# A state-space mixer with routed experts: the first drive of each tile moved from VectorE to POOL, with four reorderings around it

## The chip, the core and the metric

The kernel runs on one core of one Trainium2 chip. The metric is the device time of one execution in microseconds. Three runs of the kernel before gave 1138.83, 1135.27 and 1141.03 us; the median is 1138.83. TensorE is called PE here, VectorE DVE, ScalarE ACT, GpSimd POOL and SyncE SP.

## The reference

Sixty-four images of 3 x 96 x 96 become 37 tokens of 256 numbers each (36 patches of 16 x 16, projected, and a class token). Then come a state-space mixer and an expert layer, each with a residual and a layer norm:

```python
h = tokens(x)
h = layernorm(h + mixer(h))
h = layernorm(h + experts(h))
```

The mixer projects each token to x and z of 512 channels, runs a causal convolution of 4 taps and silu over x, and takes from it a step width per channel (`delta = softplus(...)`) and 16 numbers B and 16 numbers C per token. Then for each of 16 states s and each channel d, along the tokens of an image:

```python
h[d, s] = exp(delta[d] * A[d, s]) * h[d, s] + delta[d] * B[s] * x[d]
y[d]    = sum over s of h[d, s] * C[s]   (+ D[d] * x[d], times silu(z[d]), then projected to 256)
```

The expert layer takes the sigmoid of 32 logits per token, sums it over 8 groups of 4 experts, keeps the best 4 groups, of their experts the best 8, and adds the weighted outputs of these and of a shared expert. All is computed in 32-bit floats.

## The kernel before

**Stages.** The mixer goes over 11 tiles of up to 6 images (222 tokens; the first tile has 4 images, 148 tokens). Behind it lies the experts' stage: 179 blocks of 128 rows, gathered by expert. The change touches the mixer alone.

**A tile.** For tile i a loop runs over s = 0 to 15, one state each; I call a step of it a slot, and g = 16 i + s counts them all. In each slot:
- PE spreads row B of state g + 1 and row C of state g over 128 partitions into a bank of PSUM (`spread`, L809), two slots ahead, once the read that used the bank is done;
- ACT copies the row B from PSUM to SBUF (`copy_b`, L1076) and computes the decays, exp(delta * A), into PSUM (`decays`, L1088);
- POOL multiplies delta * x (`du`) by row B (`drives`, L629), 128 x 888 numbers, into one of four buffers;
- DVE runs the recurrence in two halves (`scan`, L1371), then multiplies the state by row C (`reads`, L1383);
- PE adds the products up over the states (`add_up`, L827).

The drive of slot 0 is the exception: DVE computes it itself (L1358), from row B in PSUM, in slot 15 of the tile before, between its scans and its read.

**What runs beside the slots.** Each engine has a function `pieces(i, s)` that says which other work it does in slot s: for the next tile n = i + 1 ("front") the convolution, softplus and so on, for the tile before t = i - 1 ("back") the output projection, layer norm, router and the allocation of rows to experts. The order of each engine's instructions is just this loop, written out by hand; semaphores tie the engines together. What matters here:
- PE: `project_patches` of tile i + 2 in slots 11 and 12 (L734), `project_z` in 12 and 14 (L790), `add_x` in 13 (L816), the convolution's parts (L748) in 14, 15 and 0; in slots 2 and 3 `project_out` of tile t, which first puts the tokens themselves (the residual) into the bank with products by the identity (L838) and then adds the projection (L845).
- ACT: in slot 12 the tanh of z, the weights of tile t (`weights`, L1156), the load of the table for the logarithm (L1193), the copy of row B of slot 15, then the logarithm of softplus (`softplus_ln`, L1068) and a line for its series (L1064).
- DVE: the router in slots 8, 9 and 10, with a copy `glist` of the four best groups (L1463); in slot 13 the smaller part (L1334), the read, `silu_z` (L1389), `tokens` of tile i + 2 (L1276) and the larger sum (`softplus_large`, L1339), which waits for ACT's logarithm; in slot 14 `softplus_sum` (L1345), which waits for POOL's product of the series, and `delta_x` (L1350), which makes `du`.
- POOL: one or more scatters of rows to DRAM in most slots (L617, tiles 2 on), the allocation's first part in slot 12 (L569 to L573) and second part in slot 14 (twelve steps that wait for each other, L576 to L587; tiles 1 on), its closing steps in slot 15 (L601 to L606), and in slot 14 the product of the series (`multiply_series`, L636), which waits for the larger sum. In a slot POOL's order is: product of the series, drive of slot g + 2, then the rest.

Of the kernel before, what the change touches and what calls it, by code (L numbers as in the profile page):

```python
# [52 lines left out]
OWN = (0,)  # L53
# [56 lines left out]
def build(nc, x, w_tok, b_tok, cls_tok, pos, w_in_x, w_in_z, conv_w, conv_b, w_x, w_dt, b_dt, a_log, d_par, w_out,  # L110
          gate_w, experts, shared, out, pool_rows, y_rows, bases):
    with ExitStack() as ctx:
# [90 lines left out]
        glist = sb("glist", [HALF, 2, 8])  # L203
# [106 lines left out]
        own_drive = sem("own_drive")  # L310
# [80 lines left out]
        CLEARED = 11  # L391
# [5 lines left out]

        def by_pool(g):
            return g % STATES not in OWN

        def pooled(g):

            return sum(by_pool(n) for n in range(g))
# [110 lines left out]
        def _(pool):  # L514
# [22 lines left out]
            for buf in (glist, gsum):  # L537
                nc.gpsimd.memset(buf[:], -2.0).then_inc(cleared, 1)
# [82 lines left out]
            def drives(g):  # L621

                i = g // STATES
                pool.wait_ge(b_copied, pooled(g + 1))
                if g % STATES == 1:
                    pool.wait_ge(du_done, i + 1)
                if g >= DRIVES:
                    pool.wait_ge(scan_done, 2 * (g - DRIVES + 1))
                nc.gpsimd.tensor_tensor(cut(drive[g % DRIVES], i), cut(du[i % 2], i),  # L629
                                        b_row[pooled(g) % B_ROWS][:, None, 0:width(i)].broadcast_to([P, KI, width(i)]), ALU.mult  # L630
# [31 lines left out]
            for i in range(-1, TILES):  # L662
                for s in range(STATES):
# [5 lines left out]
                    if 0 <= g + 2 < STATES * TILES and by_pool(g + 2):  # L669
                        drives(g + 2)  # L670
                    pieces(i, s)
# [52 lines left out]
        def _(pe):  # L724
# [70 lines left out]
            def spread(g):  # L795
# [5 lines left out]
                if g == 1:  # L801
                    pe.wait_ge(own_drive, 1)
# [28 lines left out]
            def project_out(t, b):  # L831

                h, a = half(t), images(t) // 2
                if b == 0:
                    pe.wait_ge(z2_done, 2 * t + 2)
                to = K[0:h, b * DM:(b + 1) * DM]
                for m in range(KM):
                    nc.tensor.matmul(to[:, m * P:(m + 1) * P], h0[t % 3][:, m, b * a:(b + 1) * a, :].rearrange("p a t -> p (a t)"), ident[:],  # L838
                                     start=True, stop=False, skip_group_check=True)
# [61 lines left out]
            def pieces(i, s):  # L901
# [5 lines left out]
                if i == TILES - 1 and s == 2:  # L907
                    add_x(i)
                if back and s in (2, 3):
                    project_out(t, s - 2)  # L910
# [22 lines left out]
                if i + 2 < TILES:  # L933
                    if s in (11, 12):
                        project_patches(i + 2, s - 11)
# [77 lines left out]
        def _(act):  # L1013
# [56 lines left out]
            def copy_b(g):  # L1070
# [3 lines left out]
                if pooled(g) >= B_ROWS:  # L1074
                    act.wait_ge(drive_done, pooled(g) - B_ROWS + 1)
                nc.scalar.activation(b_row[pooled(g) % B_ROWS][:, 0:w], BC[(g - 1) % 2][:, 0:w], ACT.Copy).then_inc(b_copied, 1)  # L1076
# [82 lines left out]
            def pieces(i, s):  # L1159
# [30 lines left out]
                if back and s == (12 if front else 11):  # L1190
                    weights(t)
# [586 lines left out]
```

## Time and profile before

| | |
|---|---|
| runs | 1138.83, 1135.27, 1141.03 us |
| profiled execution, own time | 1138.67 us |
| its span, first to last instruction | 1136.8 us |
| busy, share of the span | PE 87%, DVE 82%, ACT 59%, POOL 70% |
| DVE's scans L1371 | 352, 350.6 us |
| POOL's drives L629 | 165, 308.0 us |
| DVE's drives L1358 | 11, 11.3 us |

A share is an average over two stages with different limits. DVE is at nine tenths or more through nearly all of the mixer (about 40 to 775 us), PE in the experts' stage. The times of single instructions come from the timeline, which gives for each its start, its length, what it writes and reads, and, in brackets, how long its engine stood idle before it and what ended that.

### The profile page before, as it was taken

Reading aid. Unit: us, or ns where it says so; the run is one execution under the profiler, and the core shown is the slowest. Engines: PE = TensorE matmul, PEld = TensorE weight load, DVE = VectorE, ACT = ScalarE, POOL = GpSimd, SP = SyncE. Lnnn points to the kernel's source line nnn. Section 1 sums busy time; section 2 is a strip of 40 time slices with the busy share of each in tenths; the row PEclk is TensorE's granted clock in tenths of the full one; section 3 lists DMA queues with packets and bytes.
Section 4 is the critical chain, followed back from the end, with each engine's and each line's share of the span. In section 5 each row is a group of like instructions: output and inputs, shape, how many; then the busy total and the mean of one; then the engine's idle time right before and its main releaser. Section 6 shows DMA issues by size and latency. Waiting matters only on the chain.

```text
span 1136.8 us, 16973 instructions
## 1 busy us (share of the span) xinstructions
PE 987.1 (87%) x4739; PEld 755.5 (66%) x4739; DVE 935.5 (82%) x1813; ACT 672.6 (59%) x1780; POOL 793.6 (70%) x840
## 2 busy tenths in 40 slices
PE   5698889989898998989989897866699999999990
PEld 5686667767676766667767673534488888888880
DVE  4589999999999999999999999895244677777774
ACT  3575665756557575666756657541266666666661
POOL 2244577878888787888878888786501776767775
PEclk9999999999999999999999998878699999999995
DMA  5699300201111020110201010058465888889983
GB/s 187 219 326 325 114 24 23 62 15 59 38 47 55 19 82 15 54 42 31 75 14 59 14 49 28 28 214 351 147 183 176 256 263 262 261 261 273 268 260 108
DMA packets 104475, 150.28 MB, mean 132 GB/s; under 512 B 13983, under 2 KB 91231, under 8 KB 103999
## 3 DMA queue, kind: packets, MB, share of 16 engines
q1 hardware_dynamic: 87487, 107.39, 29.5%
q0 software_dynamic: 16896, 41.80, 12.7%
q8 instruction: 40, 0.66, 0.2%
q14 instruction: 52, 0.43, 0.1%
HBM read 72.32 MB, written 76.82 MB: 131 GB/s over the span
## 4 chain that ended last, share of the span: by engine, by line
DVE 30%; PE 29%; issue 17%; ACT 5%; POOL 5%; DMA 4%; SPq 2%; DVEq 0%; POOLq 0%; ACTq 0%
DVE arena L1371 17%; PE BC L983 11%; DMA mixer_own<-pool_dram 3%; DVE arena L1383 3%; PE F L734 3%; PE Y L977 3%; PE K L997 3%; PE F L997 3%; PE Y L827 2%; POOL arena L629 1%; PE D L989 1%; POOL pool_dram L617 1%; ACT arena L1039 1%; POOL gat L685 1%; PE K L790 1%
## 5 line engine op out<-in xcount | busy, mean ns | idle before, releaser
L1371 DVE TENSOR_TENSOR_SCAN arena<-D,arena 128x444 f32<-128x444 f32 (+1 forms) x352 | 350.6, 1036 | 10.9 <-ACT D L1088 8.8
L827 PE MATMUL Y<-arena,ident 128*128 128x444 f32 (+1 forms) x704 | 304.3, 560 | 1.6 <-DVE arena L1383 1.6
L685 POOL DMA_INDIRECT gat<-y_dram,slot_all x176 | 177.4, 1008 | 124.6 <-DMA y_dram<-mixer_own 67.9
L617 POOL DMA_INDIRECT pool_dram<-hrow,slot_of x176 | 175.8, 999 | 45.8 <-issue 38.1
L629 POOL TENSOR_TENSOR arena<-mixer_own,arena 128x888 f32<-128x888 f32 (+1 forms) x90 | 164.2, 1825 | 56.9 <-ACT arena L1076 56.0
L1088 ACT ACTIVATE D<-mixer_own,aneg 128x216 f32<-128x216 f32 (+1 forms) x384 | 148.3, 427 | 79.7 <-DVE arena L1371 76.6
L1383 DVE TENSOR_TENSOR arena<-arena,BC 128x888 f32<-128x888 f32 (+1 forms) x176 | 184.8, 1050 | 5.4
L983 PE MATMUL BC<-arena,xt 128*128 x716 | 186.6, 384 | 0.0
L629 POOL TENSOR_TENSOR arena<-arena 128x888 f32<-128x888 f32 x75 | 143.8, 1917 | 53.0 <-ACT arena L1076 51.3
L827 PEld LDWEIGHTS Y<-arena,ident 128*128 128x128 f32 x704 | 127.5, 200 | 73.0 <-issue 68.1
L1088 ACT ACTIVATE D<-arena,aneg 128x216 f32<-128x216 f32 x320 | 126.9, 437 | 64.8 <-DVE arena L1371 64.8
L748 PEld LDWEIGHTS F<-h,arena 128*128 128x128 f32 x704 | 130.7, 197 | 28.8 <-issue 19.1
L748 PE MATMUL F<-h,arena 128*128 128x222 f32 (+3 forms) x704 | 140.2, 346 | 7.7 <-DVE h L1276 6.4
L1636 DVE SCALAR_TENSOR_TENSOR act_g<-tanh_g,BC 128x128 f32<-128x128 f32 x179 | 51.5, 288 | 107.3 <-ACT tanh_g L1224 105.8
L983 PEld LDWEIGHTS BC<-arena,xt 128*128 128x128 f32 x716 | 123.6, 193 | 9.9 <-issue 0.3
L809 PE MATMUL BC<-bc_rows,sel 96*128 96x222 bf16 (+1 forms) x352 | 63.6, 263 | 66.4 <-DVE arena L1383 66.4
L1076 ACT ACTIVATE arena<-BC 128x222 f32<-128x222 f32 (+1 forms) x165 | 56.8, 344 | 77.4 <-PE BC L809 76.4
L809 PEld LDWEIGHTS BC<-bc_rows,sel 96*128 96x128 bf16 x352 | 30.4, 98 | 98.5 <-DVE arena L1383 86.9
L977 PE MATMUL Y<-ident,mixer_own 128*128 128x128 f32 x358 | 70.0, 278 | 10.8 <-DMA mixer_own<-pool_dram 10.6
L1220 ACT ACTIVATE xt<-Y 128x256 f32<-128x256 f32 x179 | 67.4, 377 | 18.8 <-PE Y L977 18.6
L1224 ACT ACTIVATE tanh_g<-BC 128x128 f32<-128x128 f32 x179 | 49.6, 277 | 43.8 <-PE BC L983 43.8
L734 PE MATMUL F<-arena 128*128 128x216 f32 (+1 forms) x264 | 53.1, 355 | 23.4 <-ACT mixer_own L1040 8.8
(230 smaller groups left out, 1569.8 us busy)
## 6 DMA issues: line engine op xcount, KB each, us to landing
mixer_own<-pool_dram SPq DMA_DIRECT2D x179, 144.0 KB
y_dram<-mixer_own SPq DMA_DIRECT2D x179, 128.0 KB
pool_dram<-filler SPq DMA_DIRECT2D x5, 4176.0 KB, 32.0
arena<-in_experts_dram SPq DMA_DIRECT2D x1, 7680.0 KB, 23.0
arena<-in_x_dram SPq DMA_DIRECT2D x10, 648.0 KB, 4.3
pool_dram<-filler SPq DMA_DIRECT2D x1, 4896.0 KB, 35.6
arena<-in_experts_dram SPq DMA_DIRECT2D x1, 4608.0 KB, 16.1
pool_dram<-hrow,slot_of POOLq DMA_INDIRECT x176, 2.7
```

The lines of the kernel that those rows point to most:

```text
L617: nc.gpsimd.indirect_dma_start(out=pool_rows, out_offset=bass.IndirectOffsetOnAxis(ap=slot_of[q][0:r, b, k:k + 1], axis=0), in_=hrow[q][0: ...
L629: nc.gpsimd.tensor_tensor(cut(drive[g % DRIVES], i), cut(du[i % 2], i), b_row[pooled(g) % B_ROWS][:, None, 0:width(i)].broadcast_to([P, KI ...
L685: nc.gpsimd.indirect_dma_start(out=gat[0:r, k, b, :], out_offset=None, in_=y_rows[0:(blocks_by(t) - k) * P, :], in_offset=bass.IndirectOff ...
L734: mm = nc.tensor.matmul(F[:, m * np_:(m + 1) * np_], tokw[:, k, m * P:(m + 1) * P], cut_patches(patches, n)[:, k, :], start=(k == 0), stop ...
L748: nc.tensor.matmul(to.rearrange("p (a t) -> p a t", t=TOKENS)[:, :, back:], inw4[:, k, TAPS - 1 - back, c * P:(c + 1) * P], h0[n % 3][:, k ...
L809: mm = nc.tensor.matmul(BC[g % 2][:, j * N:j * N + w], sel[:, STATES * j + s, :], bc_rows[i % 2][:, 0:w], start=True, stop=True)
L827: mm = nc.tensor.matmul(Y[j][:, 0:w], ident[:], read[g % 3][:, j * w:(j + 1) * w], start=(s == 0), stop=(s == STATES - 1), skip_group_chec ...
L977: mm = nc.tensor.transpose(PX[b % 2][:, k * P:(k + 1) * P], xg[b % XG][:, k * P:(k + 1) * P], ident[:])
L983: mm = nc.tensor.matmul(PG[b % 2][:, 0:DM], xt[b % 2][:, k * P:(k + 1) * P], weights[k], start=(k == 0), stop=(k == KM - 1))
L1088: last = nc.scalar.activation(D[b][:, c * w:(c + 1) * w].rearrange("p (a t) -> p a t", t=TOKENS)[:, :, 1:TOKENS], cut(delta[i % 2], i)[:, ...
L1371: nc.vector.tensor_tensor_scan(state[g % 2][:, lo:hi], D[b][:, 0:hi - lo], drive[g % DRIVES][:, lo:hi], 0.0, ALU.mult, ALU.add).then_inc(s ...
L1383: nc.vector.tensor_tensor(cut(read[g % 3], i), cut(state[g % 2], i), BC[g % 2][:, None, N:N + width(i)].broadcast_to([P, KI, width(i)]), A ...
```

## The change

- All sixteen drives of a tile run on POOL. The one of slot 0 comes in slot 14 behind the product of the series and the second part of the allocation, and waits for `du`. ACT copies its row B too, first thing in slot 14; DVE's L1358 and its semaphore go, and its read of slot 15 now waits for that copy.
- The list for the group mask: no copy `glist`; the last four entries of `gtop` are overwritten with -2 by a memset on DVE and `gtop` itself is the list.
- DVE runs the larger sum of softplus ahead of `tokens` in slot 13.
- PE puts the residual's products of both halves into the bank in slot 0 (`add_tokens`), not in slots 2 and 3.
- The second `project_patches` goes from slot 12 to slot 13; on ACT the weights of tile t go from slot 12 to 13 and the copy of row B comes before the table load.

```diff
@@ POOL
             def drives(g):
                 i = g // STATES
-                pool.wait_ge(b_copied, pooled(g + 1))
-                if g % STATES == 1:
+                pool.wait_ge(b_copied, g + 1)
+                if g % STATES == 0:
                     pool.wait_ge(du_done, i + 1)
...
                     if i + 1 < TILES and s == 14:
                         multiply_series(i + 1)
-                    if 0 <= g + 2 < STATES * TILES and by_pool(g + 2):
+                    if s == 14:
+                        pieces(i, s)
+                    if 0 <= g + 2 < STATES * TILES:
                         drives(g + 2)
-                    pieces(i, s)
+                    if s != 14:
+                        pieces(i, s)
@@ PE
+            def add_tokens(t):
+
+                h, a = half(t), images(t) // 2
+                pe.wait_ge(z2_done, 2 * t + 2)
+                for b in range(2):
+                    for m in range(KM):
+                        nc.tensor.matmul(K[0:h, b * DM + m * P:b * DM + (m + 1) * P],
+                                         h0[t % 3][:, m, b * a:(b + 1) * a, :].rearrange("p a t -> p (a t)"), ident[:],
+                                         start=True, stop=False, skip_group_check=True)
...
+                if back and s == 0:
+                    add_tokens(t)
                 if back and s in (2, 3):
                     project_out(t, s - 2)
...
-                    if s in (11, 12):
-                        project_patches(i + 2, s - 11)
+                    if s in (11, 13):
+                        project_patches(i + 2, (s - 11) // 2)
@@ ACT
-                if back and s == (12 if front else 11):
+                if back and s == (13 if front else 11):
                     weights(t)
                 if front and s == 12:
-                    nc.scalar.preload_act_table_set("natural_log_exp_and_others")
                     if mix:
                         copy_b(STATES * i + s + 3)
+                    nc.scalar.preload_act_table_set("natural_log_exp_and_others")
                     softplus_ln(n)
@@ DVE
                 if b == 0:
-                    if by_pool(g):
-                        dve.wait_ge(drive_done, pooled(g + 1))
-                    else:
-                        dve.wait_ge(own_drive, g + 1 - pooled(g + 1))
+                    dve.wait_ge(drive_done, g + 1)
...
-                in_turn(nc.vector.tensor_copy(glist[0:h, :, 0:TOPG], gtop[0:h, :, 0:TOPG]))
+                in_turn(nc.vector.memset(gtop[0:h, :, TOPG:], -2.0))
                 for b in range(2):
                     hold()
-                    last = nc.vector.match_replace(gleft[0:h, b, :], glist[0:h, b, :], gsum[0:h, b, :], -1.0)
+                    last = nc.vector.match_replace(gleft[0:h, b, :], gtop[0:h, b, :], gsum[0:h, b, :], -1.0)
...
+                if front and s == 13:
+                    softplus_large(n)
                 if i + 2 < TILES and s == 13 and mix:
                     tokens(i + 2)
-                if front and s == 13:
-                    softplus_large(n)
...
-                    if 0 <= g + 1 < STATES * TILES and not by_pool(g + 1):
-                        drives(g + 1)
                     if 0 <= i < TILES:
                         reads(g)
```

## Rows read from the trace of the kernel before

**Rows 1.** Busy us per engine by stretch: length, PE, PEld, DVE, ACT, POOL, granted clock, DMA.

```profile
492.00:560.00 68.00, 62.04 (x286) 46.02 (x285) 66.14 (x96) 43.14 (x111) 56.88 (x60) 0.97 0.15 45
800.00:1137.00 337.00, 300.18 (x1613) 247.42 (x1611) 206.22 (x702) 194.16 (x559) 199.23 (x202) 0.95 0.77 228
```

**Rows 2.** Timeline of DVE, one tile's slots 8 to 15: start, us, what, idle before.

```profile
467.69 0.94 DVE L1463 COPY glist<-gtop 111x8 f32<-111x8 f32 x1
...
491.18 2.29 DVE L1339 SCALAR_TENSOR_TENSOR arena<-arena,ln_small 128x888 f32<-128x888 f32 x1 [0.30 <-ACT arena L1068]
...
496.65 1.14 DVE L1345 SCALAR_TENSOR_TENSOR arena<-arena,ln_small 128x888 f32<-128x888 f32 x1
...
500.78 1.05 DVE L1358 TENSOR_TENSOR arena<-arena,BC 128x888 f32<-128x888 f32 x1
...
503.27 2.04 DVE L1371 TENSOR_TENSOR_SCAN arena<-D,arena 128x444 f32<-128x444 f32 x2
```

**Rows 3.** Timeline of POOL in the same slots.

```profile
466.70 1.91 POOL L629 TENSOR_TENSOR arena<-mixer_own,arena 128x888 f32<-128x888 f32 x1 [0.83 <-ACT arena L1076]
...
485.43 1.93 POOL L629 TENSOR_TENSOR arena<-mixer_own,arena 128x888 f32<-128x888 f32 x1 [0.20 <-ACT arena L1076]
...
490.60 1.93 POOL L629 TENSOR_TENSOR arena<-mixer_own,arena 128x888 f32<-128x888 f32 x1
492.70 1.63 POOL L617 DMA_INDIRECT pool_dram<-hrow,slot_of  x1 [0.16 <-issue]
494.35 2.08 POOL L636 TENSOR_TENSOR arena<-arena 128x888 f32<-128x888 f32 x1
...
496.71 1.23 POOL L577 TENSOR_SCALAR new_off<-new_off 128x32 f32<-128x32 f32 x1
498.03 0.98 POOL L578 TENSOR_TENSOR off_diff<-old_off,new_off 128x32 f32<-128x32 f32 x1
...
502.48 1.93 POOL L629 TENSOR_TENSOR arena<-arena 128x888 f32<-128x888 f32 x1
```

**Rows 4.** Timelines of PE and ACT there and in slots 15 to 2.

```profile
487.21 2.35 PE L734 MATMUL F<-arena 128*128 128x216 f32 x12
489.40 0.35 PE L809 MATMUL BC<-bc_rows,sel 96*128 96x222 bf16 x2
490.04 1.03 ACT L1068 ACTIVATE arena<-arena,one_col 128x888 f32<-128x888 f32 x1
...
503.12 3.20 PE L827 MATMUL Y<-arena,ident 128*128 128x444 f32 x4
...
509.65 0.36 ACT L1076 ACTIVATE arena<-BC 128x222 f32<-128x222 f32 x1 [3.50 <-PE BC L809]
514.08 0.60 PE L838 MATMUL K<-ident,h 128*111 128x128 f32 x4
```

**Rows 5.** Busy us of PE alone in a short stretch: length, busy, granted clock, DMA.

```profile
503.00:506.00 3.00, 3.00 (x6) 0.51 0.00 0
```

**Rows 6.** Timelines of DVE and POOL at the ends of tiles 1 and 2.

```profile
149.72 1.91 POOL L629 TENSOR_TENSOR arena<-arena 128x888 f32<-128x888 f32 x1 [1.00 <-POOL fresh L573]
150.63 1.95 DVE L1339 SCALAR_TENSOR_TENSOR arena<-arena,ln_small,mixer_own 128x888 f32<-128x888 f32 x1 [0.30 <-ACT arena L1068]
160.89 1.90 POOL L629 TENSOR_TENSOR arena<-mixer_own,arena 128x888 f32<-128x888 f32 x1
162.37 2.04 DVE L1371 TENSOR_TENSOR_SCAN arena<-D,arena 128x444 f32<-128x444 f32 x2
...
212.61 1.93 POOL L629 TENSOR_TENSOR arena<-mixer_own,arena 128x888 f32<-128x888 f32 x1 [0.39 <-ACT arena L1076]
229.05 0.32 POOL L587 TENSOR_TENSOR slot<-slot,chosen 111x64 f32<-111x64 f32 x1
230.45 2.04 DVE L1371 TENSOR_TENSOR_SCAN arena<-D,arena 128x444 f32<-128x444 f32 x2
```

**Rows 7.** Timeline of DVE, the list's copy behind the last tile.

```profile
789.27 0.29 DVE L1463 COPY glist<-gtop 111x8 f32<-111x8 f32 x1
```

## What I expect, worked out before the run

> **What bounds the kernel now.** I read the share of each engine by stretch first. In a tile of the mixer (68 us) VectorE (DVE) is busy 66.1 us, TensorE (PE) 62.0, POOL 56.9 and ACT 43.1 [rows 1], and in DVE's timeline the rows follow each other almost without a gap [rows 2], so DVE sets the length of a tile. Behind the mixer lies the experts' stage of 337 us, where PE is busy 300 us [rows 1]; the change touches nothing there, so what the mixer gains or loses moves the end one for one. Then I read POOL's timeline alone. From 466.70 in slot 8 to the drive at 502.48 POOL has work queued without a break: the only wait for another engine in that stretch is 0.20 us, at 485.43 [rows 3]. The same wait of 0.18 to 0.21 us stands in each of the tiles 3 to 9. So in the second half of a tile POOL is full too, and it is there that the change adds to it.
>
> I call tile i's step s "slot s"; its scans are DVE's L1371, and the length of a tile is the distance between the first scans of two tiles (435.08 to 503.27 in the tile shown, 68.2 us).
>
> **Drive of slot 0 from DVE to POOL.** DVE drops L1358, 1.05 us at 500.78 [rows 2], ten full ones and a short one of 0.76. On POOL the same product takes 1.92 us (the row behind the allocation, 502.48) [rows 3]. Its place is the question. POOL runs the product of the series (494.35, 2.08 us), then the twelve steps of the allocation's second part, and ends them at 502.5 [rows 3]. Two of these steps, 1.23 and 0.98 us at 496.71 and 498.03 [rows 3] where their neighbours take 0.25, coincide with DVE's two softplus products, which follow each other from 496.65 on [rows 2], which read two operands from SBUF: POOL stands while DVE reads. That cost remains, since DVE's sum needs POOL's product and is released just as the allocation begins. In the new order the drive follows: 502.5 + 1.93 = 504.4, and DVE can scan from about 504.5 (handing over took 0.1 us at such places). Before, the scan began at 503.27 [rows 2]. Without its drive DVE is ready 1.05 us earlier, at 502.2, and stands 2.3 us. Net: +1.24 us for this boundary. What is queued behind the waiting scan on DVE is the read, the gating of the tile before and slot 1; ACT's decays and PE's sums hang on the scan. POOL catches up afterwards: the drive of slot 1 follows at 504.4 to 506.3 and that of slot 2 behind the closing steps at about 510.5, and the scans that take them come at about 509 and 512.
>
> **List of groups by memset.** The copy glist (L1463) takes 0.94 us at 467.69 [rows 2] and 0.29 at the end, with only scatters on POOL [rows 7]. It ends with POOL's drive of 466.70 + 1.91 [rows 3]: it waits for it. A memset of 8 numbers reads nothing; I bound it by 0.1 (the size of the smallest rows) and by the copy's own 0.94, and take 0.2. The mask that follows is also a fast scalar operation and may now meet the same drive, so I count 0.6 us, not 0.75. The Trainium skill (SBUF — State Buffer, Who interferes with whom) says that copies and scalar operations in the two-port modes take the port pair that VectorE shares with GpSimd, and that a VectorE instruction with at most one SBUF input outside these modes does not; the copy's row agrees, and no run here shows the memset. Were the memset to wait as the copy does, the sum below would be 2.1 us higher. But where does the 0.6 us go? POOL's stretch began at 466.70, before it, and does not end sooner because DVE is early; only the wait of 0.20 us at 485.43 can vanish, since ACT's copy before it follows DVE. So 0.2 of the 0.6 counts in tiles 3 to 9. In tiles 1 and 10 POOL has gaps or no drive to deliver, and all of it counts.
>
> **PE and ACT around slot 12.** PE's second projection of patches (2.35 us at 487.21) stands ahead of the spread at 489.40, on which ACT's copy of B waits, and the logarithm begins at 490.04 [rows 4]. Moved behind the spread, and with the weights (0.5 us) moved to slot 13, the copy comes before the table load, and the logarithm starts about 0.4 us sooner, 1.0 with what DVE gained before: it ends at about 490.0 to 490.6. The moved projection now stands before the spread of slot 13; since that of slot 12 came out of the way, PE reaches it with the same work done as before: nothing. Tokens need the projection, and the larger sum between covers it.
>
> **Larger sum ahead of tokens.** L1339 takes 2.29 us [rows 2]; its sister L1345 takes 1.14. It starts at 491.18, POOL's drive runs from 490.60 to 492.53, and it ends 0.95 us after that [rows 2, 3]: it waits for POOL. Tokens (0.66 us) now run behind it. If it starts while the drive runs, it still ends at 493.45, and DVE is 0.66 us later for the two softplus products and scan 15, at 503.0 instead of 502.2, still before 504.5. If it starts before the drive, the drive starts 0.7 us late, but the scatter behind (1.63 us at 492.70 against 1.0 of the others) no longer meets it and shrinks by about as much. Either way POOL reaches the product of the series at 494.2 to 494.4: 0 to -0.15 us; I take 0.
>
> **Residual's products in slot 0.** Four products per tile, in two pairs of 0.60 us as the one at 514.08 [rows 4], go to slot 0. There PE is slow: after a wait of 2.24 us for DVE its sums take 3.20 us, and ACT's copy at 509.65 waits 3.50 us for PE [rows 4]; the granted clock was 0.51 there, the lower level of 1.2 GHz [rows 5]; the decay of slot 2 is ready at 510.7 and its scan starts at 510.8. So 0.6 to 1.1 us more there would be felt if nothing else moved. But this chain begins at the read of slot 15, which ends up to 1.05 us sooner, while DVE's first scan comes 1.2 us later: 2 us of cover. I take 0 and keep +0.5 per tile as the upper bound.
>
> **The sum,** against the profiled execution's 1138.67 us (its span 1136.8 and 1.9 around it; the median of the three runs is 1138.83, practically the same):
> - boundaries behind tiles 3 to 9: 7 x (1.24 - 0.20) = +7.3.
> - behind tile 2: POOL's allocation ends at 229.37, so the scan comes at 231.36 against 230.45, +0.9; POOL's waits of 0.39 at 212.61 [rows 6] and 0.19 before that may go: +0.35.
> - behind tile 1: no scatters. POOL's drive at 149.72 and the sum at 150.63 move up about 0.9 us by the earlier copy of B, so the drive that stands at 160.89 ends at about 161.8; the scan was at 162.37 [rows 6]: -0.5, and -0.2 for the list: -0.7.
> - behind tile 0: no allocation, POOL has been idle for microseconds; L1358, 1.05 there too, goes entirely: -1.05, and -0.1 for the earlier sum: -1.15.
> - into tile 0: POOL takes its short drive (1.23 us) right behind du, ending when DVE's did: 0.
> - tile 10: the list -0.7; the last tile -0.15.
>
> Together +4.95: **1143.6 us**.
>
> **Rivals.**
> A, the forecast: POOL's chain sets each tile's start. With the unknowns (the 0.2, the 0.15, handing over, memset, 0.5 per tile on PE for part of the tiles) its own range is 1140 to 1148. For it: seven tiles with the same rows. 0.55.
> B, POOL is relieved so far that DVE's savings arrive: the meetings with DVE vanish from POOL's stretch (0.98 + 0.73 in the allocation, 0.65 in the scatter, 0.3 in its first part: 2.7 us). Then the drive ends at 501.6, DVE is ready at 502.2 minus 0.6; with PE's chain of slot 0 taking 0.6 back, 9 x (-1.05) and -3 for tiles 0, 10 and the list: 1126. It would need the softplus products to fall outside the allocation, against which their order speaks. 0.10.
> C, the sum L1339 starts over 0.6 us before the drive that it now waits for, when the scatter ahead still runs, so that neither drive nor later scatter is held: POOL's stretch shortens by 0.65, 8 x 0.65 = 5.2: 1138.4, no change. It decides if the logarithm ends before 489.5; I get 490.0. "Issue order, not op shape, decides who blocks", says the Trainium skill on the same page and section; no run here shows this order. 0.17.
> D, slower still: the sum takes the port just before the drive of slot 15, which slips by 0.7 us, and the scatter keeps its 1.63: 8 x 0.7 = +5.6, 1149.2. It decides when L1339 begins within the 0.6 us before that drive. 0.18.
> That the memset is no faster than the copy lies within A.
>
> **Numbers.** A measurement of this kernel can tell about 0.5% from no change (5.7 us, so 1144.5). A gives slower in a little under half of its cases, D always, C nearly never, B faster: faster 0.12, same 0.45, slower 0.43. The range leaves out most of B and the outer tails: 1135 to 1150.
>
> **What would show it.** Right: a wait of DVE's L1371 for POOL's L629 of 1.5 to 2.4 us at nine boundaries, tiles of about 69.2 us, and the slot's first drive ending 1.9 us behind the last step of the allocation. The list under 0.3 us shows that part. Wrong: no such wait, or a tile at 67 us (B); scatters of slot 13 at 1.0 us with drives of slot 15 that are not longer (C), or with drives at 2.6 us and later products (D); waits of L1371 for ACT in slot 2 (PE's part).

## The result, and the profile after

The changed kernel took 1143.14 us in the median of 22 runs (1139.29 to 1149.21), the kernel before 1139.70 in 22 runs beside it (1134.88 to 1145.06). The ratio is 1.0037, with a 95% interval of 1.0025 to 1.0049: 4.2 us slower (the two medians lie 3.4 us apart), clear of noise, but less than the 0.5% that I had called no change. The forecast was 1143.6 us. The number is right; the working behind it is right where a tile ends and wrong where it begins, as the trace shows.

The profiled execution took 1143.08 us, its span 1141.3 (before 1138.67 and 1136.8). Busy shares hardly move: PE 86%, DVE 81%, ACT 59%, POOL 71%. In the changed kernel DVE's scan is L1356, its read L1368, the larger sum L1336, softplus_sum L1342 and tokens L1273; POOL's drive is L617, its scatter L606, its allocation L565 to L576; PE's spread is L800, `add_up` L818, `add_tokens` L828; ACT's copy of row B is L1073.

**The boundary between two tiles.** The tile that answers to the one of [rows 2, 3] begins with the scan at 436.49. Timeline of POOL there, after (start, us, what, idle before and what ended it):

```profile
467.10 1.91 POOL L617 TENSOR_TENSOR arena<-mixer_own,arena 128x888 f32<-128x888 f32 x1 [0.85 <-ACT arena L1073]
...
481.48 1.91 POOL L617 TENSOR_TENSOR arena<-mixer_own,arena 128x888 f32<-128x888 f32 x1 [0.21 <-ACT arena L1073]
...
486.08 1.93 POOL L617 TENSOR_TENSOR arena<-mixer_own,arena 128x888 f32<-128x888 f32 x1 [0.33 <-ACT arena L1073]
...
491.25 1.92 POOL L617 TENSOR_TENSOR arena<-mixer_own,arena 128x888 f32<-128x888 f32 x1
493.33 1.62 POOL L606 DMA_INDIRECT pool_dram<-hrow,slot_of  x1 [0.16 <-issue]
494.98 2.08 POOL L624 TENSOR_TENSOR arena<-arena 128x888 f32<-128x888 f32 x1
...
498.06 1.04 POOL L568 TENSOR_TENSOR new_off<-new_off,seen 128x32 f32<-128x32 f32 x1
499.19 1.07 POOL L569 TENSOR_SCALAR full_rows<-nblocks 128x32 f32<-128x32 f32 x1
...
502.73 0.32 POOL L576 TENSOR_TENSOR slot<-slot,chosen 111x64 f32<-111x64 f32 x1
503.01 3.78 POOL L617 TENSOR_TENSOR arena<-arena 128x888 f32<-128x888 f32 x2
```

And of DVE:

```profile
468.88 0.07 DVE L1448 MEMSET gtop<- 111x8 f32 x1
...
491.31 2.80 DVE L1336 SCALAR_TENSOR_TENSOR arena<-arena,ln_small 128x888 f32<-128x888 f32 x1 [0.36 <-ACT arena L1065]
494.04 0.66 DVE L1273 TENSOR_TENSOR h<-F,posb 128x216 f32<-128x216 f32 x2
...
505.02 2.05 DVE L1356 TENSOR_TENSOR_SCAN arena<-D,arena 128x444 f32<-128x444 f32 x2 [1.30 <-POOL arena L617]
```

The slot's first drive stands right behind the last step of the allocation (the row at 503.01 holds it and the next drive), and DVE's first scan waits 1.30 us for it. The forecast's sign of being right, such a wait, stands at nine boundaries, if shorter than the 1.5 to 2.4 us that I had given: 0.59 behind tile 1, 1.30 or 1.31 behind tiles 2 to 8, 1.97 behind tile 9. From the end of the allocation to the scan are 2.0 us, where before it was 0.8 [rows 2, 3]. POOL's stretch from slot 8 to the end of the allocation (taken at the start of the drive behind it) is 35.9 us in this tile (before 35.8) and 35.6 in the two tiles ahead of it.

**The other end of the tile.** From the first scan to the start of POOL's stretch there were 31.6 us before (435.08 to 466.70); now 30.6 (436.49 to 467.10). That holds in four of the tiles 2 to 9 (tiles 4 to 7). In the other four it is 32.0 to 32.3.

The 1.0 us that the first kind gains is nearly all in slots 2 and 3. PE's spreads in slots 1, 2 and 3, before, then after:

```profile
442.76 0.36 PE L809 MATMUL BC<-bc_rows,sel 96*128 96x222 bf16 x2 [1.34 <-DVE arena L1383]
...
448.12 0.36 PE L809 MATMUL BC<-bc_rows,sel 96*128 96x222 bf16 x2
...
451.98 0.35 PE L809 MATMUL BC<-bc_rows,sel 96*128 96x222 bf16 x2
...
444.03 0.36 PE L800 MATMUL BC<-bc_rows,sel 96*128 96x222 bf16 x2 [3.40 <-DVE arena L1368]
...
448.95 0.36 PE L800 MATMUL BC<-bc_rows,sel 96*128 96x222 bf16 x2
...
452.38 0.36 PE L800 MATMUL BC<-bc_rows,sel 96*128 96x222 bf16 x2
```

They stood 5.36 and 3.86 us apart and now stand 4.92 and 3.43 apart: a pair of the residual's products (0.60 us) is gone from each stretch, and 0.87 us with them. The spread of slot 1 itself comes 7.68 us behind the first scan before and 7.54 after.

What makes the second kind stands in PE's timeline at slot 1. A tile of the first kind, then one of the second, both after (the row of eight matmuls is the sums of slots 0 and 1, four products; a product of 32-bit floats counts as two):

```profile
512.56 0.36 PE L800 MATMUL BC<-bc_rows,sel 96*128 96x222 bf16 x2 [3.39 <-DVE arena L1368]
512.76 3.16 PE L818 MATMUL Y<-arena,ident 128*128 128x444 f32 x8
...
581.17 0.36 PE L800 MATMUL BC<-bc_rows,sel 96*128 96x222 bf16 x2 [3.41 <-DVE arena L1368]
581.38 4.85 PE L818 MATMUL Y<-arena,ident 128*128 128x444 f32 x8
```

The same wait of 3.4 us, the same sums, but 3.16 us in one and 4.85 in the other. The granted clock of the two stretches (windows of all engines, after: stretch, length, PE, PEld, DVE, ACT, POOL, clock, DMA):

```profile
512.50:516.00 3.50, 3.44 (x12) 1.93 (x13) 3.46 (x5) 2.19 (x6) 1.66 (x2) 1.00 0.02 5
581.20:586.00 4.80, 4.80 (x10) 2.38 (x11) 4.77 (x6) 2.35 (x7) 2.80 (x3) 0.64 0.00 0
```

In the second the clock was at its lower level of 1.2 GHz for most of the stretch. POOL feels it two drives later, through ACT's copy of row B (timeline of POOL, after, a tile of each kind):

```profile
518.32 1.92 POOL L617 TENSOR_TENSOR arena<-arena 128x888 f32<-128x888 f32 x1 [0.51 <-ACT arena L1073]
...
588.62 1.93 POOL L617 TENSOR_TENSOR arena<-mixer_own,arena 128x888 f32<-128x888 f32 x1 [2.19 <-ACT arena L1073]
```

So the tiles come out in two lengths, and none has the 69.2 us of the forecast. First scan to first scan, before and after, with what I had forecast for the difference ("both": the sum of the two tiles; "falls" and "held" are PE's clock in slot 1, after):

| tile | before | after | difference | forecast |
|---|---|---|---|---|
| up to the first scan | 42.29 | 43.59 | +1.30 | 0 |
| 0 | 52.78 | 50.96 | -1.82 | -1.15 |
| 1 | 67.30 | 66.45 | -0.85 | -0.70 |
| 2 (clock falls) | 68.08 | 69.64 | +1.56 | +0.35 |
| 3 (falls) | 68.17 | 69.46 | +1.29 | +1.04 |
| 4, 5 (held) | 68.24, 68.22 | 68.18, 68.21 | -0.07 both | +2.08 both |
| 6, 7 (held) | 68.19, 68.13 | 68.53, 68.61 | +0.82 both | +2.08 both |
| 8, 9 (falls) | 68.05, 68.03 | 69.78, 69.68 | +3.38 both | +2.08 both |
| tile 10 and the rest | | | -1.1 | -0.85 |
| span | 1136.8 | 1141.3 | +4.5 | +4.95 |

### The profile page after: what moved, and what is told of

It reads as the page before. It is cut to its first block, busy times and chain, and to the rows that moved or that the text cites. A ratio compares the mean times of both kernels' runs of the same rounds, so it can differ in the third digit from the quotient of the medians.

```text
span 1141.3 us, 17003 instructions
## 1 busy us (share of the span) xinstructions
PE 982.9 (86%) x4739; PEld 752.4 (66%) x4739; DVE 924.8 (81%) x1802; ACT 676.0 (59%) x1791; POOL 809.1 (71%) x850
## 4 chain that ended last, share of the span: by engine, by line
POOL 37%; PE 26%; issue 16%; DVE 10%; ACT 5%; DMA 4%; SPq 1%; POOLq 0%; DVEq 0%; ACTq 0%
POOL arena L617 17%; PE BC L980 11%; POOL pool_dram L606 9%; DVE arena L1356 5%; DMA mixer_own<-pool_dram 3%; PE Y L974 3%; PE F L994 3%; PE K L994 3%; POOL arena L624 2%; PE F L739 2%; PE Y L818 2%; POOL gat L676 1%; PE D L986 1%; ACT D L1085 1%; DVE arena L1368 1%
## 5 line engine op out<-in xcount | busy, mean ns | idle before, releaser
L1356 DVE TENSOR_TENSOR_SCAN arena<-D,arena 128x444 f32<-128x444 f32 (+1 forms) x352 | 351.1, 1037 | 26.1 <-POOL arena L617 15.1
L818 PE MATMUL Y<-arena,ident 128*128 128x444 f32 (+1 forms) x704 | 299.8, 554 | 1.6 <-DVE arena L1368 1.6
L676 POOL DMA_INDIRECT gat<-y_dram,slot_all x176 | 174.3, 990 | 126.4 <-DMA y_dram<-mixer_own 70.2
L617 POOL TENSOR_TENSOR arena<-mixer_own,arena 128x888 f32<-128x888 f32 (+1 forms) x96 | 174.5, 1823 | 49.9 <-ACT arena L1073 46.9
L606 POOL DMA_INDIRECT pool_dram<-hrow,slot_of x176 | 175.4, 996 | 45.5 <-issue 38.0
L1368 DVE TENSOR_TENSOR arena<-arena,BC 128x888 f32<-128x888 f32 (+1 forms) x176 | 184.9, 1051 | 5.7
L617 POOL TENSOR_TENSOR arena<-arena 128x888 f32<-128x888 f32 x80 | 152.9, 1916 | 45.8 <-ACT arena L1073 42.0
L818 PEld LDWEIGHTS Y<-arena,ident 128*128 128x128 f32 x704 | 127.0, 200 | 73.3 <-issue 68.5
L800 PE MATMUL BC<-bc_rows,sel 96*128 96x222 bf16 (+1 forms) x352 | 63.2, 262 | 75.4 <-DVE arena L1368 75.1
L800 PEld LDWEIGHTS BC<-bc_rows,sel 96*128 96x128 bf16 x352 | 29.4, 98 | 107.7 <-DVE arena L1368 97.1
L1073 ACT ACTIVATE arena<-BC 128x222 f32<-128x222 f32 (+1 forms) x176 | 60.0, 341 | 60.5 <-PE BC L800 60.5
L1217 ACT ACTIVATE xt<-Y 128x256 f32<-128x256 f32 x179 | 67.2, 375 | 18.4 <-PE Y L974 18.4
```

The source lines that it names most:

```text
L606: nc.gpsimd.indirect_dma_start(out=pool_rows, out_offset=bass.IndirectOffsetOnAxis(ap=slot_of[q][0:r, b, k:k + 1], axis=0), in_=hrow[q][0: ...
L676: nc.gpsimd.indirect_dma_start(out=gat[0:r, k, b, :], out_offset=None, in_=y_rows[0:(blocks_by(t) - k) * P, :], in_offset=bass.IndirectOff ...
L800: mm = nc.tensor.matmul(BC[g % 2][:, j * N:j * N + w], sel[:, STATES * j + s, :], bc_rows[i % 2][:, 0:w], start=True, stop=True)
L818: mm = nc.tensor.matmul(Y[j][:, 0:w], ident[:], read[g % 3][:, j * w:(j + 1) * w], start=(s == 0), stop=(s == STATES - 1), skip_group_chec ...
L1356: nc.vector.tensor_tensor_scan(state[g % 2][:, lo:hi], D[b][:, 0:hi - lo], drive[g % DRIVES][:, lo:hi], 0.0, ALU.mult, ALU.add).then_inc(s ...
L1368: nc.vector.tensor_tensor(cut(read[g % 3], i), cut(state[g % 2], i), BC[g % 2][:, None, N:N + width(i)].broadcast_to([P, KI, width(i)]), A ...
```

## Experiments

The kernels ran on three chips, in the order below: the first four on one where the kernel before takes 1261.8 us, the next four where it takes 1138.5, the last four where it takes 1264.8. The traces put the difference behind the mixer: from tile 10's first scan to the end they show 427 to 433 us on the second chip and 550 to 560 on the other two, while tiles 4 and 5 are 68.2 us long in the changed kernel and, where the clock held, 68.2 to 68.3 in its variants on the others. So each ratio below is against the kernel before on the same chip, and beside it I give the **nine tiles**: the time from DVE's first gating product of tile 1 to that of tile 10, in the one trace of each kernel. It is 612.4 us before (68.0 per tile) and 618.6 after.

Three theories. P: POOL's chain alone sets the tile, as forecast. Q: the clock alone makes the difference. R: a tile is the sum of two terms; PE's chain in slots 1 to 8, at the clock that is granted, sets when POOL's stretch begins, and POOL's stretch with the drive behind it sets when the next tile does.

### The four reorderings alone

The kernel before with the list by memset, the sum ahead of tokens, the residual's products in slot 0 and the moves of slots 12 and 13; L1358 stays on DVE.

> The four reorderings alone; DVE keeps its drive of slot 0. Theory P (POOL's chain through the allocation and the drive behind it sets each tile's start): the wait of 1.30 us before the tile's first scan goes, DVE's drive of 1.05 us comes back, DVE is ready about 0.25 us sooner per tile than in the changed kernel: 1140 to 1142 us. Rival Q (PE's granted clock and PE's chain through slots 0 to 3 set the tile, POOL's wait fills slack): PE waits 1 us longer in slot 15, its clock falls at the start of every tile as before, and nothing is gained: 1143 to 1145 us.

Ratio 1.0031 [1.0000, 1.0062], nine tiles 614.2. No gain at all: PE waits 2.69 us in slot 15 (before 2.24) and its clock falls there at the seven boundaries behind tiles 2 to 8, as before. POOL's stretch begins at 31.2 to 31.6 in tiles 3 to 9: what the residual's products free in slots 2 and 3 is lost again in slots 15 and 0, where they now stand behind the slow sums. PE's timeline, this kernel:

```profile
503.08 0.55 PE L807 MATMUL BC<-bc_rows,sel 96*128 96x222 bf16 x2 [2.69 <-DVE arena L1387]
```

### The drive alone

The reverse: `drives` of slot 0 on POOL behind the allocation, all else as before.

> The drive of slot 0 on POOL behind the allocation alone; list, order of sum and tokens, residual's products, patches and ACT's order as before. P: nine boundaries 1.24 us later, one 1.05 sooner: 1149 us. Q: the wait for POOL takes the place of DVE's drive and of slack, time follows the clock: 1139 to 1142 us.

Ratio 1.0229 [1.0184, 1.0275], nine tiles 642.7: 71.4 us per tile, far over what a chain of POOL alone gives. DVE waits 1.97 for POOL, which costs 1.2 as forecast; the rest comes from PE (its timeline, this kernel, slot 1 of one tile):

```profile
456.69 0.55 PE L802 MATMUL BC<-bc_rows,sel 96*128 96x222 bf16 x2 [3.95 <-DVE arena L1364]
457.03 5.46 PE L820 MATMUL Y<-arena,ident 128*128 128x444 f32 x8
```

It waits 3.95 us and is slow afterwards, in each of the tiles 2 to 9. POOL waits 3.1 to 3.6 us for a copy of row B, and its stretch begins 33.7 to 34.0 us behind the first scan. P falls.

### The drive in the middle of the allocation

```diff
 # POOL, allocation, second part, behind its sixth step
+                if t < TILES - 2:
+                    drives(STATES * (t + 2))
```

and not behind it. Otherwise the changed kernel.

> The changed kernel with POOL's drive of slot 0 behind the sixth of the twelve steps of the allocation's second part, when du is just ready. P: DVE finds the drive done, the wait of 1.30 us goes at nine boundaries: 1143 - 11.7 = 1131.5 us. Q: at most 3 us of it arrive: 1140 us or more.

Ratio 0.9972 [0.9941, 1.0003], nine tiles 608.2. DVE's wait for POOL is gone. PE now waits 2.00 us in slot 1, and the clock falls in five tiles of eight. Tiles where it held take 66.8 to 67.2 us, where it fell 67.8 to 68.7. PE's timeline in it, slot 1 of a tile of each kind:

```profile
508.44 0.55 PE L802 MATMUL BC<-bc_rows,sel 96*128 96x222 bf16 x2 [2.01 <-DVE arena L1370]
508.78 4.70 PE L820 MATMUL Y<-arena,ident 128*128 128x444 f32 x8
...
576.82 0.36 PE L802 MATMUL BC<-bc_rows,sel 96*128 96x222 bf16 x2 [2.00 <-DVE arena L1370]
577.01 3.16 PE L820 MATMUL Y<-arena,ident 128*128 128x444 f32 x8
```

### PE kept busy in slot 1

```diff
+                if back and s == 1:
+                    for _ in range(3):
+                        add_tokens(t)
                 if back and s in (2, 3):
```

12 further products on PE (24 matmuls of the trace), which write the same values again, in the changed kernel. They add work and shorten no chain.

> The changed kernel with the residual's products computed four times over in slots 0 and 1 (the same values into the same place), so that PE has 3.1 us of work where it stood 3.4 us. P: no change, 1142 to 1144 us. Q: the granted clock stays full in every tile; the four tiles of 69.6 us become 68.2 and the time falls by 5 to 6 us, to 1137.5.

Ratio 1.0006 [0.9976, 1.0036], nine tiles 613.1. The clock is 1.00 in the first 12 us of every tile (1 to 9). PE's timeline, this kernel:

```profile
506.88 1.04 PE L828 MATMUL K<-ident,h 128*111 128x128 f32 x8
507.75 0.35 PE L800 MATMUL BC<-bc_rows,sel 96*128 96x222 bf16 x2
507.95 2.78 PE L828 MATMUL K<-ident,h 128*111 128x128 f32 x24
511.52 0.36 PE L800 MATMUL BC<-bc_rows,sel 96*128 96x222 bf16 x2 [0.79 <-DVE arena L1371]
511.72 3.16 PE L818 MATMUL Y<-arena,ident 128*128 128x444 f32 x8
```

With 2.8 us more of work for PE in each tile the nine tiles are 5.5 us shorter than after. (The two ratios can't be told apart by their intervals; this reading rests on the traces.) DVE still waits 1.31 for POOL at each boundary. So the two terms are separate: this takes away one of them alone.

### The sum of slot 0 ahead of the spread

```diff
+                    if 0 <= i < TILES and s == 1:
+                        add_up(g - 1)
                     if -1 <= g + 2 < STATES * TILES and g != -2:
                         spread(g + 2)
                     if 0 <= i < TILES:
-                        if s == 1:
-                            add_up(g - 1)
```

In slot 1 of the changed kernel PE no longer holds the sum of slot 0 back behind a spread that waits for DVE's read.

> The changed kernel with PE's sum of slot 0 ahead of the spread of slot 1 and nothing else. R: the clock does not fall and PE's chain behind the wait is 1.5 us shorter; the stretch begins at 30.6 or sooner in all tiles, the wait for POOL of 1.3 us stays: nine tiles in 608 to 613 us (618.6 in the changed kernel), ratio 0.997 to 1.001. P: as the changed kernel, 1.004.

Ratio 0.9976 [0.9957, 0.9994], nine tiles 612.7. PE's wait shrinks to 1.50 us, the sums of slots 0 and 1 come one by one, and the clock holds in slot 1 of tiles 1 to 9:

```profile
511.35 0.36 PE L800 MATMUL BC<-bc_rows,sel 96*128 96x222 bf16 x2 [1.50 <-DVE arena L1368]
511.55 1.67 PE L818 MATMUL Y<-arena,ident 128*128 128x444 f32 x4
```

Its nine tiles are those of the experiment before, without extra work. It is one reordered step that makes up what the change had cost.

### Both: the drive in the middle and the sum early

> The drive of slot 0 within the allocation, and PE's sum of slot 0 ahead of the spread of slot 1, where PE stands 3.4 us. Theory R (two terms: POOL's chain sets a tile's start, and PE's chain through slots 1 to 8, at whichever granted clock, sets when POOL's full stretch begins): no wait for POOL, full clock in every tile, the stretch begins 30 us or less into a tile, tiles of 66.8 us or less, nine tiles in 602 us where before has 612.4: ratio 0.990 to 0.993. Theory P (POOL's chain alone): as with the drive in the middle alone, ratio 0.997.

1125.41 us against 1138.51, ratio 0.9882 [0.9859, 0.9905], nine tiles 601.4 (66.8 each). The best kernel of the study. Lines from its timeline, of POOL, then DVE, then PE:

```profile
489.91 0.25 POOL L570 TENSOR_TENSOR full_rows<-full_rows,seen 128x32 f32<-128x32 f32 x1
490.24 1.91 POOL L619 TENSOR_TENSOR arena<-arena 128x888 f32<-128x888 f32 x1
492.11 0.32 POOL L573 TENSOR_TENSOR in_old<-rank,full_rows 111x64 f32<-111x64 f32 x1
...
493.20 2.05 DVE L1358 TENSOR_TENSOR_SCAN arena<-D,arena 128x444 f32<-128x444 f32 x2
...
500.73 0.36 PE L802 MATMUL BC<-bc_rows,sel 96*128 96x222 bf16 x2 [0.50 <-DVE arena L1370]
500.93 1.67 PE L820 MATMUL Y<-arena,ident 128*128 128x444 f32 x4
```

The drive ends 1.0 us before DVE wants it, the scan has no wait, PE waits 0.5 us.

### Residual's products back in slots 2 and 3

> The changed kernel with the residual's products back in slots 2 and 3. R: PE stands over 4 us in slot 1, its clock falls in every tile, and 1.2 us of products return to its chain: the stretch begins near 33.9, tiles of 71.5 us, ratio 1.02. P (and my forecast, which took 0 for this part): the changed kernel's time, 1.004.

Ratio 1.0231 [1.0205, 1.0256], nine tiles 638.8. PE waits 3.95 us in slot 1 where it waited 3.4 (the products in slot 0 that filled 0.55 us of it are gone), the clock falls in each tile, and two pairs of products stand in the chain of slots 2 and 3 (PE's timeline, this kernel):

```profile
452.16 0.55 PE L800 MATMUL BC<-bc_rows,sel 96*128 96x222 bf16 x2 [3.96 <-DVE arena L1362]
452.50 5.75 PE L818 MATMUL Y<-arena,ident 128*128 128x444 f32 x8
458.09 0.60 PE L829 MATMUL K<-ident,h 128*111 128x128 f32 x4
...
461.95 0.60 PE L829 MATMUL K<-ident,h 128*111 128x128 f32 x4
```

POOL's stretch begins at 33.0 us in tile 2, 33.2 in tile 3 and 34.1 to 34.2 from there on. This is the part I had taken at 0. It has two terms: the spreads of slots 1 to 3 stand 0.87 us further apart, as before the change, which makes 7 to 8 us; the other 12 to 13 of the 20 us that the nine tiles lose are the clock's, by subtraction.

### Larger sum back behind tokens

> The changed kernel with tokens ahead of the larger sum again. R and the forecast: DVE waits for POOL anyway in slot 0, so nothing: 1.003 to 1.005, the wait for POOL 0.6 us longer. Rival S (the order sets when POOL gets the product of the series): 1 us per tile either way, 1.012 or 0.996.

Ratio 1.0169 [1.0143, 1.0195], nine tiles 631.6, against an expectation near 1.004: a miss. I had thought of the order as a matter of POOL's port; it is one of who waits. In this kernel tokens meet PE's moved projection (DVE's timeline), and the first scan waits 1.97 for POOL:

```profile
504.85 0.67 DVE L1273 TENSOR_TENSOR h<-F,posb 128x216 f32<-128x216 f32 x2 [1.00 <-PE F L725]
...
518.00 2.05 DVE L1356 TENSOR_TENSOR_SCAN arena<-D,arena 128x444 f32<-128x444 f32 x2 [1.97 <-POOL arena L617]
```

Since tokens no longer stand between the sum and softplus_sum, DVE stands before the first scan 0.67 us longer, and PE, which follows DVE through slots 15 and 0, waits 3.95 us in slot 1 instead of 3.4. The clock then falls in every tile, and POOL's stretch begins at 32.0 to 33.6.

### The copy of the list back

> The changed kernel with the list by copy again. The forecast took 0.2 us per tile for the memset: 1.005. R: the copy takes 0.9 us, DVE comes 0.85 us later to slot 15, so the wait for POOL is 0.5 us instead of 1.3 and PE stands 2.6 us in slot 1 instead of 3.4: its clock holds in all tiles, which begin POOL's stretch at 30.6: nine tiles in 613 us, ratio 0.998 to 1.000, the slower operation being no loss.

Ratio 1.0115 [1.0080, 1.0151], nine tiles 623.9, expected 0.998 to 1.000 by R and 1.005 by the forecast: a miss. PE was to wait 2.6 us in slot 1 and DVE 0.5 at the boundary; they wait 3.40 and 1.30 as in the changed kernel. The copy itself costs little. DVE's timeline, this kernel, two tiles:

```profile
404.63 0.21 DVE L1450 COPY glist<-gtop 111x8 f32<-111x8 f32 x1
...
542.48 0.96 DVE L1450 COPY glist<-gtop 111x8 f32<-111x8 f32 x1
```

The tiles in which the clock held take 68.30 and 68.31 us, against 68.18 and 68.21 after: 0.1 us. In its trace the clock fell in four of the seven tiles that wait 3.4 us, and one of these is 71.2 long, where the changed kernel has three of seven and none over 69.8. Its profiled execution, 1272.96 us, is the fastest of its six; four of the others lie at 1280.5 to 1281.3. More falls would explain those, but no trace of them exists: why this kernel should lose 1% stays open.

### ACT's order and the second projection back

> The changed kernel with the second projection of patches in slot 12, ACT's weights there too and the table load ahead of the copy of B. R and the forecast: the larger sum starts 0.6 us later, still while POOL's drive runs, and ends where it did: no change in the tiles with a held clock, 1.003 to 1.005. Rival: the drive of slot 15 waits for its copy of B and POOL's chain grows: 1.008 or more.

Ratio 1.0037 [1.0010, 1.0063], that of after. The larger sum starts 55.3 us behind the first scan and not 54.8, waits for POOL's drive and takes 2.28 us instead of 2.80, so that it ends where it did, and the held tiles 6 and 7 are 68.53 and 68.62 long, as after. The moves bring the logarithm 0.5 us forward and the tile nothing. (Its trace had five falls of seven, and nine tiles of 624.8; that execution was 3 us over its median.)

### The larger sum behind tokens, in the best kernel

> As the kernel with the drive within the allocation and the early sum (0.9882), with tokens ahead of the larger sum again. With no wait for POOL left, DVE's time decides: the larger sum waits for POOL's drive of slot 15 either way, so tokens ahead of it are free: 0.6 us per tile, nine tiles in 596 us, ratio 0.983 to 0.985. If the product of the series on POOL decides instead: no change, 0.988.

Ratio 0.9894 [0.9857, 0.9931], nine tiles 602.2, where I expected 0.984: a miss. Tokens wait 1.00 us for PE's moved projection, but the larger sum takes 1.59 us instead of 2.82, and DVE reaches the first scan 0.6 us sooner. The scan of slot 2 then waits 0.69 us for POOL's drive, in each of the tiles 3 to 9, where the best kernel has no such wait; that eats what the order frees. DVE's timeline, this kernel:

```profile
486.67 0.67 DVE L1275 TENSOR_TENSOR h<-F,posb 128x216 f32<-128x216 f32 x2 [1.00 <-PE F L727]
...
505.96 2.05 DVE L1358 TENSOR_TENSOR_SCAN arena<-D,arena 128x444 f32<-128x444 f32 x2 [0.69 <-POOL arena L619]
```

### The best kernel without the four reorderings

The kernel before with the drive on POOL in the middle of the allocation and the sum of slot 0 ahead of the spread, nothing else.

> The kernel before with the drive of slot 0 on POOL within the allocation and the early sum of slot 0 on PE, without the list, the order of the larger sum, the residual's products and the order around slot 12. R: DVE loses its 1.05 us per tile and waits for nothing new, PE's chain has 1.5 us less and keeps its clock in slot 1: nine tiles in 603 us, ratio 0.990 to 0.993. If the four reorderings are needed for the gain: 1.000 or more.

Ratio 0.9907 [0.9877, 0.9936], nine tiles 603.1. Once the clock holds and the drive comes in time, the four reorderings together are worth 1.7 us by the traces (the intervals of the two ratios overlap); where PE waits at slot 1, the residual's products alone decide over 20.

### The two terms, side by side

Length of a tile in us, in the traces of the changed kernel (tiles 4 and 5 held, 8 and 9 fell) and of the kernels with the drive in the middle (4, 5 and 8 held with the early sum, 4 and 5 fell without it):

| | clock held in slot 1 | clock fell |
|---|---|---|
| drive behind the allocation | 68.2 | 69.7 |
| drive in the middle of it | 66.9 | 68.4 |

Each term is worth the same whatever the other does: 1.3 us for the drive's place, 1.5 for the clock. The clock's is not one size: where the slow sums took 5.7 to 6.0 us and not 4.4 to 4.9, in the kernels with the list or ACT's order back, the tile was 70.7 to 71.2 us long. R stands, and P and Q each name half; but R doesn't say which tiles lose the clock, and there its expectations missed twice (larger sum back, list back).

## Why the prediction came out as it did

**POOL's stretch sets the next tile: right.** The drive follows the allocation at once, hand-over included the scan comes 2.0 us behind its end, and the boundary costs 2.01 - 0.79 = 1.22 us against a forecast 1.24. I had the scan at "about 504.5" in the old tile's time; the wait was 1.30 and not 1.5 to 2.4, because DVE arrived later than I had it: its larger sum took 2.80 us and tokens stand behind it, which I gave as the later of my two cases for DVE. For the boundary nothing hangs on that, as DVE is not what ends last there. For PE it does: with the wait at 1.97, as in the kernel with the larger sum back, PE waits 3.95 us and loses its clock in every tile.

**The race for the port: neither C nor D.** The drive began at 491.25 and the larger sum at 491.31; the drive won by 0.06 us, so the sum took 2.80 where it had taken 2.29 [rows 2], and the scatter behind it kept its 1.62 (before 1.63 [rows 3]). In the allocation the two slow steps are now L568 and L569, 1.04 and 1.07, where before they were L577 and L578, 1.23 and 0.98 [rows 3]: DVE's two softplus products (L1342 and L1347) meet other steps, at the same price. "That cost remains" held, and B with it fell.

**The wait of 0.20 that should vanish: half right.** In tiles 4 and 5 the stretch is 35.56 us, 0.22 shorter, as forecast. In tiles 6 and 7 it is 35.9 and 36.0, with waits of 0.21 to 0.33 for ACT's copy.

**The list: right in kind.** The memset takes 0.07 us in every tile, a little under the 0.1 that I had as its lower bound, and what reached the tile was 0.1 and not 0.2. The Trainium skill (SBUF — State Buffer, Who interferes with whom) says that VectorE's copies in the two-port modes and GpSimd shut each other out; the copy's rows agree: in tiles 2 to 9 of the kernel with the list back it ends 0.03 us behind POOL's drive, and is 0.95 to 0.97 us long or 0.20 to 0.21, by when in the drive it began. No memset here was held, even where the drive ran beside it.

**The start of POOL's stretch: the term that was missing.** My sum took the 31.6 us between the first scan and POOL's stretch as given, and added the change behind it. It is made by PE, and the change moved it both ways. Before, PE waited 2.24 us in slot 15 and its clock fell there at the seven boundaries behind tiles 2 to 8 [rows 4, 5]; the row of the slow sums, 3.20 us, was in my list, and I used it only to price four products. After, that wait is 1.84 and the same sums take 1.67 at a clock of 1.00 (windows: 503.00 to 506.00). By itself that was worth little: in tile 2 before, where the clock held, the stretch began at 31.5, and at 31.5 to 31.6 in the tiles behind it. It let the residual's products run in slot 0 at full clock, so that their 0.87 us in slots 2 and 3 came out as a gain; with the four reorderings alone, where the clock fell in slot 15, it did not. Together that brings 1.0 us per tile, which the forecast lacks. But DVE's first scan comes later and waits for POOL, PE has done its work of slots 15 and 0 early, and now stands 3.4 us in slot 1; there the clock falls in about every second tile, and in such a tile the stretch begins 1.4 to 1.7 us later. Tiles 3 to 9 came to +5.4 where I had +7.3; tile 2, where I had +0.35, to +1.56, for the same reason. With the start-up these errors nearly cancel; that the forecast lay 0.5 us off the measured median is in part luck.

**Residual's products in slot 0: the step that failed.** I wrote "I take 0" with +0.5 as the upper bound, and asked only whether they delay the chain in slot 0. Undone, they cost 22 us more (1.0231 against 1.0037): they stand in the chain of slots 2 and 3 again, 0.87 us a tile, and no longer fill 0.55 us of PE's wait, which decides the clock. Both ends of my range, 0 and +0.5, left out a gain; the rows that spoke for one were the pair of products in slot 2 and the sums of slot 15 at half clock behind 2.24 us of idling [rows 4, 5].

**Start-up and ends.** The first scan came 1.3 us later, 1.0 of which was there already at the larger sum of tile 0 (37.71 for 36.73), ahead of anything that the change touches; 0.3 is the drive on POOL, where I had 0. Tile 0 gave 1.8 back for a forecast 1.15, tile 10 and the rest 1.1 for 0.85. These rows can't be read closer than that: the kernel with the sum early and the one with the drive in the middle too run the same instructions up to the end of tile 0, and it takes 52.2 us in one trace and 49.4 in the other.

## What to carry to other kernels

When an engine's step is moved off the bounding engine, ask not only when the receiver delivers, but which third engine will stand idle because of it, and what that one does first afterwards: with the drive moved alone, DVE's wait cost 1.2 us a tile and PE's fallen clock behind it 2.2 (its sums took 5.46 us for 3.16). A stage's start is a term of the sum like its end; if the profile shows a matmul row at twice its usual length right behind a wait, each edit that lengthens, shortens or fills that wait has a price, up or down, even if it lies beside the critical chain. Put a late product as early in its engine's queue as its inputs allow, in the middle of a block of small steps rather than behind it.

## What was not expected of the hardware

How often the granted clock fell behind a wait of PE for DVE, over the traces of all kernels (tiles 2 to 9; waits of 1.5 us and more that recur in a place, and one contrary case; by whether the sums behind it took 3.2 us or less for eight, 1.7 for four, or markedly longer):

| wait before the sums | where | fell |
|---|---|---|
| 1.50 | slot 1 | none of 7 |
| 1.84 | slot 15 | none of 56, in eight kernels |
| 2.00 | slot 1 | 6 of 9 |
| 2.24 | slot 15 (before) | 7 of 7 |
| 2.69 | slot 15 | 7 of 7 |
| 2.69 | slot 1 | 3 of 3 |
| 2.88 | slot 1 (before) | none of 1 |
| 3.40 | slot 1 | 13 of 22 |
| 3.95 | slot 1 | 21 of 21 |

It doesn't go by the length of the wait alone: 2.24 us always lost the clock in slot 15, where 3.40 in slot 1 lost it in a little over half, and what PE did ahead of it differs between the two. In tile 1, not in the table, it fell behind 1.85 us in slot 1 in two kernels of six. In one kernel the tiles with the same rows ahead fell or not, and in runs (changed kernel: 2 and 3 fell, 4 to 7 held, 8 and 9 fell), so these are not independent cases; a single trace tells only its own execution, and a ratio of such a kernel is a mean over both kinds.

An indirect DMA on POOL (the scatter) took 1.62 us beside DVE's larger sum, which reads two operands from SBUF, and 0.9 to 1.2 elsewhere. And the same kernel took 11% longer on two other chips; in the traces of its variants nearly all of it lies in the experts' stage, at a granted clock of 0.84 there against 0.94.
